# A graph kernel's opening: row statistics on ScalarE, row 0 placed ahead of the turnings of h0

## What is computed

```python
h = jnp.maximum(_layernorm(x, axis=-1), 0.0)
x = x + L0(h)       # three edge convolutions and a closing projection
h = jnp.maximum(_layernorm(x, axis=-1), 0.0)
x = x + L1(h)       # one weighted aggregation, normalised over the nodes

def _layernorm(x, axis=-1, eps=1e-05):
    m = jnp.mean(x, axis=axis, keepdims=True)
    v = jnp.var(x, axis=axis, keepdims=True)
    return (x - m) / jnp.sqrt(v + eps)

def _edge_conv(x, src, dst, W, b):
    xi = x[dst]
    xj = x[src]
    m = jnp.concatenate([xi, xj - xi], axis=-1) @ W + b
    s = jax.ops.segment_sum(m, dst, num_segments=N)
    cnt = jax.ops.segment_sum(jnp.ones((dst.shape[0],), m.dtype), dst, num_segments=N)
    return s / jnp.maximum(cnt, 1.0)[:, None]
```

## Time and profile before

| | us |
|---|---|
| median of 3 runs | 111.09 (110.65 to 111.28) |
| the profiled execution | 111.21 |
| its span | 109.4 |
| TensorE busy | 98.6 (90%) |
| its weight loads | 91.8 (84%) |
| VectorE busy | 87.9 (80%) |
| ScalarE busy | 63.8 (58%) |
| GpSimd busy | 20.8 (19%) |

### The profile page before, as it was taken

One profiled execution on the slowest core, in us unless ns is written; L12 is line 12 of the kernel. 1 busy time (PEld: TensorE's weight loads), 2 busy tenths in 40 slices (PEclk: granted clock), 3 DMA queues, 4 the chain that ended last, 5 costly groups with the idle time before them and its releaser, 6 DMA issues.

```text
span 109.4 us, 2712 instructions
## 1 busy us (share of the span) xinstructions
PE 98.6 (90%) x1050; PEld 91.8 (84%) x1050; DVE 87.9 (80%) x257; ACT 63.8 (58%) x154; POOL 20.8 (19%) x27
## 2 busy tenths in 40 slices
PE   0395999979999999999999999999999999999950
PEld 0333898867799989999999999999999999999840
DVE  2589999999999998999953599940999989808960
ACT  1595999998699989302858133557513153423540
POOL 7200000000000059100399920192000000000000
PEclk9999999999999999999999999999999999999999
DMA  1984930000030000000050200000000000000035
GB/s 28 260 186 93 328 115 0 0 6 3 3 99 0 6 0 9 6 0 3 0 192 13 88 0 0 6 0 0 0 6 0 0 0 0 0 0 6 0 76 158
DMA packets 7008, 4.63 MB, mean 42 GB/s; under 512 B 2175, under 2 KB 6994, under 8 KB 6994
## 3 DMA queue, kind: packets, MB, share of 16 engines
q1 hardware_dynamic: 6068, 3.68, 12.4%
q10 hardware_dynamic: 926, 0.75, 2.6%
HBM read 3.79 MB, written 0.64 MB: 40 GB/s over the span
## 4 chain that ended last, share of the span: by engine, by line
PE 72%; DVE 17%; DMA 5%; issue 1%; ACTq 1%; ACT 0%; DVEq 0%
PE bank L1385 14%; PE bank L1286 12%; PE bank L1142 12%; PE bank L1143 11%; PE bank L1144 11%; DVE src_hot L591 8%; DMA x_in<-in_x_dram 5%; PE bank L1216 4%; PE bank L1423 2%; PE bank L1363 2%; DVE stats L544 2%; DVE stats L864 1%; PE bank L1468 1%; DVE x_in L895 1%; DVE dst_hot L587 1%
## 5 line engine op out<-in xcount | busy, mean ns | idle before, releaser
L591 DVE TENSOR_SCALAR src_hot<-node_id,edge_cols 125x626 f16<-125x626 f16 x77 | 23.6, 379 | 0.0
L1286 PE MATMUL bank<-dst_hot,src_hot 125*128 125x84 f16 (+6 forms) x505 | 20.1, 195 | 1.3 <-DVE src_hot L591 1.1
L1286 PEld LDWEIGHTS bank<-dst_hot,src_hot 125*128 125x128 f16 x505 | 18.8, 98 | 2.8 <-DVE src_hot L591 1.8
L1385 PE MATMUL bank<-counts,u_lo 125*128 125x312 f32 (+3 forms) x60 | 16.7, 308 | 0.0
L1068 ACT ACTIVATE h_hi<-pre 128x312 fp32r<-128x312 f32 (+1 forms) x12 | 5.6, 466 | 16.4 <-DVE pre L757 16.4
L1385 PE MATMUL bank<-counts,u_hi 125*128 125x312 f32 (+3 forms) x48 | 14.0, 307 | 0.0
L1143 PE MATMUL bank<-wf_hi,h_lo 128*125 128x256 f32 x40 | 11.3, 281 | 0.0
L1142 PE MATMUL bank<-wf_hi,h_hi 128*125 128x256 f32 x40 | 11.3, 281 | 0.0
L1144 PE MATMUL bank<-wf_lo,h_hi 128*125 128x256 f32 x40 | 11.2, 281 | 0.0
L1385 PEld LDWEIGHTS bank<-counts,u_lo 125*128 125x128 f32 (+1 forms) x60 | 11.0, 189 | 0.0
L1003 ACT ACTIVATE parts<-bank 125x250 f32<-125x250 f32 x25 | 10.2, 411 | 0.0
(11 more groups left out here) (144 smaller groups left out, 250.0 us busy)
## 6 DMA issues: line engine op xcount, KB each, us to landing
raw<-in_L_gnn_W_dram SPq DMA_DIRECT2D x3, 512.0 KB, 6.6
x_in<-in_x_dram ACTq DMA_DIRECT2D x1, 560.0 KB
raw<-in_L_gnn_Wf_dram SPq DMA_DIRECT2D x1, 512.0 KB, 3.7
out_dram<-x_in SPq DMA_DIRECT2D x2, 168.0 KB
wf<-in_L_gnn_Wf_dram SPq DMA_DIRECT2D x1, 256.0 KB, 7.6
raw<-in_L_gnn_Wf_dram SPq DMA_DIRECT2D x1, 256.0 KB, 2.7
raw<-in_L_gnn_W_dram SPq DMA_DIRECT2D x1, 256.0 KB, 2.7
out_dram<-x_in SPq DMA_DIRECT2D x2, 112.0 KB
```

The lines of the kernel that those rows point to most:

```text
L591: dve.tensor_scalar(src_hot[:, t % RING, 0:IDS], node_id[:, 0:IDS], edge_cols[:, 0, t:t + 1], None, ALU.is_equal).then_inc(src_hot_vector, 1)
L1286: return pe.matmul(built[s][:, :, n0:n0 + n], src_hot[:, t % RING, BLK * s:BLK * s + P], dst_hot[:, c, :, j // 2, c0:c0 + n, j % 2], start ...
L1385: ins = pe.matmul(bank[KF * h + f][:, 0:e - a], u[0:n, k, P * f:P * (f + 1)], counts[0:n, k, a:e], start=False, stop=(k == NB - 1 and u is ...
```

## The change

- The statistics of x leave VectorE. ScalarE makes them with two activations a block that also write the sum of their output over the row: a copy scaled by 256^-1.5, whose sum is the mean over 16, and a square of (that mean minus x / 16), whose sum is the variance. They write their elements into `h0`, which is overwritten later. The shift is then made with -16 in place of -1.
- Source tiles 4, 22 and 27 are made by VectorE in place of ScalarE.
- On VectorE the reciprocal and the shift stand ahead of tile 15 (`NORM_AT`) in place of behind tile 1; the deviations come ahead of tile 9 in place of tile 5.
- TensorE places the whole of row 0 first. Behind it come the turnings 0, 1, 2, the products of blocks 0 and 1, the turnings 3 and 4, and the other products.
- Five warming products in place of ten.
- `centre` in the closing statistics waits for one count less, since the variances of x raise that semaphore no more.

```diff
@@ -62,9 +62,10 @@
 EPS = 1e-5
 
 FULL = 112
-SCALAR_EARLY, SCALAR_NEXT, SCALAR_LATER = (0, 4), (22, 27), {0: (34, 38), 1: (52,), 2: (71,)}
-SCALAR_TILES = SCALAR_EARLY + SCALAR_NEXT + sum(SCALAR_LATER.values(), ())
-DEV_AT, BAD_AT, VECS_AT, DIFF_AT = 5, 13, 26, 33
+SCALAR_EARLY, SCALAR_LATER = (0,), {0: (34, 38), 1: (52,), 2: (71,)}
+SCALAR_TILES = SCALAR_EARLY + sum(SCALAR_LATER.values(), ())
+DEV_AT, BAD_AT, VECS_AT, DIFF_AT = 9, 13, 26, 33
+NORM_AT = 15
 U_AT = (30, 38, 42)
 FLAG_AT = 62
 
@@ -324,6 +325,8 @@
         parts_copied = sem("parts_copied")
         weights_summed = sem("weights_summed")
         variance_ready = sem("variance_ready")
+        row_mean_ready = sem("row_mean_ready")
+        row_variance_ready = sem("row_variance_ready")
         std_ready = sem("std_ready")
         norm_ready = sem("norm_ready")
         h0_ready = sem("h0_ready")
@@ -550,14 +553,14 @@
                     last = dve.bn_aggr(moments[0:BLK, b, :], stats[0:BLK, b, :])
                 last.then_inc(variance_ready, 1)
 
-            def scale_shift(blocks, ready):
+            def scale_shift(blocks, ready, by=-1.0):
 
                 stds[0] += 1
                 dve.wait_ge(std_ready, stds[0])
                 lo, hi = blocks[0], blocks[-1] + 1
                 step.add(dve.reciprocal(rstd[0:BLK, lo:hi], rstd[0:BLK, lo:hi]))
                 step.wait()
-                dve.scalar_tensor_tensor(out=shift[0:BLK, lo:hi], in0=moments[0:BLK, lo:hi, 0], scalar=-1.0,
+                dve.scalar_tensor_tensor(out=shift[0:BLK, lo:hi], in0=moments[0:BLK, lo:hi, 0], scalar=by,
                                          in1=rstd[0:BLK, lo:hi], op0=ALU.mult, op1=ALU.mult).then_inc(ready, 1)
 
 
@@ -624,14 +627,10 @@
             dve.tensor_copy(weight_parts[:, :, :, 0:PER], p2).then_inc(weight_parts_ready, 1)
             dve.wait_ge(weight_parts_ready, 1)
             weighted_window(0)
-            dve.wait_ge(x_loaded, 32)
-            for b in range(NB):
-                moments_of(b)
-            variances(range(NB))
             dve.wait_ge(edge_cols_ready, 1)
-            source_tile(1)
-            scale_shift(range(NB), norm_ready)
-            for t in range(2, TILES):
+            for t in range(1, TILES):
+                if t == NORM_AT:
+                    scale_shift(range(NB), norm_ready, -math.sqrt(D))
                 if t == DEV_AT:
                     deviations()
                 if t == BAD_AT:
@@ -870,7 +869,7 @@
                             stats[:, 2 * f:2 * f + 2, :].rearrange("p a b -> p (a b)")).then_inc(variance_ready, 1)
 
             def centre(f):
-                dve.wait_ge(variance_ready, stds[0])
+                dve.wait_ge(variance_ready, stds[0] - 1)
                 step.add(dve.scalar_tensor_tensor(out=shift[:, f:f + 1], in0=moments[:, f, 0:1], scalar=vec(3, f),
                                                   in1=vec(3, f), op0=ALU.add, op1=ALU.subtract))
                 step.wait()
@@ -976,17 +975,25 @@
                 copy(h0_t[:, :, BLK * b:BLK * (b + 1)], t2).then_inc(h0_t_ready, 1)
 
 
-            root(rstd[0:BLK, 0:NB], moments[0:BLK, 0:NB, 1])
+            act.wait_ge(x_loaded, 32)
+            for b in range(NB):
+                nc.scalar.activation(h0[:, b, :], x_in[:, b, :], ACT.Copy, scale=D ** -1.5,
+                                     accum_out=moments[0:BLK, b, 0:1]).then_inc(row_mean_ready, 1)
+            for i, b in enumerate(range(NB)):
+                act.wait_ge(row_mean_ready, i + 1)
+                nc.scalar.activation(h0[:, b, :], x_in[:, b, :], ACT.Square, bias=moments[0:BLK, b, 0:1],
+                                     scale=-D ** -0.5, accum_out=moments[0:BLK, b, 1:2]).then_inc(row_variance_ready, 1)
+            act.wait_ge(row_variance_ready, NB)
+            nc.scalar.activation(rstd[0:BLK, 0:NB], moments[0:BLK, 0:NB, 1], ACT.Sqrt,
+                                 bias=eps[0:BLK, :]).then_inc(std_ready, 1)
             act.wait_ge(norm_ready, 1)
             for b in range(NB):
                 nc.scalar.activation(h0[:, b, :], x_in[:, b, :], ACT.Relu, bias=shift[0:BLK, b:b + 1],
                                      scale=rstd[0:BLK, b:b + 1]).then_inc(h0_ready, 1)
                 if 1 <= b < NB - 1:
                     h0_high(b - 1)
-            source_tile(SCALAR_NEXT[0])
             h0_high(NB - 2)
             h0_high(NB - 1)
-            source_tile(SCALAR_NEXT[1])
             high_rows(("u", 0, 0), 0, 2)
 
             def copy_block(r, s):
@@ -1170,7 +1177,7 @@
             ins.then_inc(filled, 1)
             pe.wait_ge(constants_ready, 3)
             pe.wait_ge(padding_ready, 1)
-            keep_warm(10)
+            keep_warm(5)
 
             def turn_dev():
                 pe.wait_ge(bad_ready, 1)
@@ -1261,8 +1268,6 @@
                 return pe.matmul(o[:, 0:e - a], degree_r[0:rows, :], part[0:rows, NB - 1, a:e], start=opens, stop=closes,
                                  skip_group_check=True)
 
-            jobs = {2: (0,), 4: (1,), 6: (2,), 9: (3, 4)}
-            assert max(jobs) < len(window_pieces(0))
             made = [0, 0]
 
             def wait_tile(t):
@@ -1290,10 +1295,6 @@
                 if r == 0:
 
                     for i in range(len(pieces)):
-                        if i == 8:
-                            neighbour_terms_0(U0_BLOCKS[:1])
-                        for b in jobs.get(i, ()):
-                            turn_h0(b)
                         wait_tile(seen)
                         seen += 1
                         for s in range(NB):
@@ -1322,6 +1323,11 @@
                             pe.wait_ge(flag_ready, 1)
                             general = pe.value_load(flag[0:1, 0:1], min_val=0, max_val=1)
                 if r == 0:
+                    for b in range(3):
+                        turn_h0(b)
+                    neighbour_terms_0(U0_BLOCKS[:1])
+                    turn_h0(3)
+                    turn_h0(4)
                     neighbour_terms_0(U0_BLOCKS[1:])
                 if r == 1:
                     own_terms_0()
```

## The result

The changed kernel takes **115.09 us** (median of 4, 114.95 to 115.14), the kernel before 110.89 in the same comparison: ratio 1.0367, 95% interval 1.0343 to 1.0391. It is slower, as forecast, but by 4.2 and not by 2.1, and lies 0.3 above the range. The profiled execution takes 115.14, its span is 113.0, 2.14 lie around it.

What follows compares the result with a forecast made beforehand. TensorE, busy for 90% of the span, was taken to bound the kernel; row 1 ending at 26.65 instead of 24.54 adds 2.1 to 111.21, giving 113.3, or 113.2 against the median 111.09; range 111.8 to 114.8 us.

Steps and rivals of the forecast that it cites:

- The direction and its mechanism: TensorE, opening: 5.63 of turnings and products left behind row 0, idle 0.87 and 0.37 for ScalarE's copies; 2.1 us slower.
- the first h0: ScalarE, after its statistics and the root: first h0 at 12.86 instead of 10.06.
- Writing the sum ... I take 0.15, ten times, 1.5: ScalarE's statistics: writing sums costs 0.15 each, 1.5 in all (0 to 3.0), on top of 3.35 for the activations.
- TensorE's clock: Rival, TensorE's opening: 1.2 GHz, hidden in row 0; 118.8 us if it lasts through turnings and products; chance 0.05.
- all 5.63 doubled: Clock rival's price: the turnings and products behind row 0, 5.63 of work, double at the low level, giving 118.8.
- Five end at 7.5. That is worth nothing in itself: TensorE's start: five warming products end at 7.5, no gain in itself, since row 0 goes at VectorE's pace.
- The chain after 24.54 shows no such room: After the own terms' old start: argument that nothing later can make up part of the 2.1 delay.
- the third rival: Something later, such as row 4, takes up at most 1.0: 112.2, or about 111.4 with cheap sums; chance 0.05.
- The time around the span: Outside the profiled span: 1.8 of the kernel before's 111.21; the forecast added only the 2.1 to that whole time.
- The stall at t = 15: VectorE at the normalisation: idle about 0.9, from 11.5 to 12.4, waiting for ScalarE's root.
- that for the high part of u: VectorE after its tiles at 18.3: idle about 1.9 until ScalarE has the high part of u of block 0.
- The wait for tile 34: TensorE in row 1: waits 0.35 for ScalarE's tile 34, ready at 24.75.

Runs made afterwards that it cites:

- the filled standstill: The changed kernel with seven unused products of 512 columns ahead of TensorE's wait for tile 15: 112.74 us, ratio 1.0152 to the kernel before.
- thicker placements: The changed kernel with one unused product of 256 columns ahead of each of tiles 2 to 14: 114.22 us, ratio 1.0297 to the kernel before.
- the order alone: The kernel before with row 0 placed ahead of the turnings and products, statistics, tiles and ten warming products as before: 116.89 us, ratio 1.0484.
- the same order: The changed kernel with turnings 0 and 1 ahead of tile 15 and turning 2 ahead of tile 17: 112.24 us, ratio 1.0117; 111.25 at clock 1.0.

## Why the prediction was wrong

- **The direction and its mechanism were right.** TensorE is behind with 5 turnings and 10 products when row 0 ends, and the copies in ScalarE's queue hold it up. At full clock (the filled standstill) the own terms start 1.6 later, where 2.1 was forecast; the 0.5 between them comes from the first h0, which is there 0.6 sooner than forecast.
- **"Writing the sum ... I take 0.15, ten times, 1.5"** was too dear: 0.09, so 0.9. With the last 0.1 and x landing 0.2 sooner, the first h0 came at 12.25, not 12.86, and row 0 ended at 14.65, not 15.2. Without the readings the activations are 0.31 and 0.40 apart; my 0.28 and 0.39 from the rows were a little low. The trace agrees with what I had estimated from the figures of the Trainium skill ("ScalarE: Activation LUTs", "What ACT_TABLE_LOAD costs"), 0.31 and 0.40.
- **The step that failed is "TensorE's clock", chance 0.05, "against it: the idle stretches before cost nothing".** What the runs show in its place is a fall to 1.2 GHz, from 14.0 to 20.8 in the profiled execution and with a mean clock of 0.97 in all four, worth 2.3 of the 4.2; the rival at 0.05 was the one that came. The idle stretches before did cost nothing, but there products of fp32 operands stood between them. The change takes out exactly these, and half of the warming products, and puts 4.5 of thin placements and a standstill of 1.67 in their place. The times that make the standstill stood in my working (VectorE at its wait until 12.4, then the windows), and I did not lay them beside the clock. The price was put at the extreme too, all 5.63 doubled; measured, the low level covered the turnings and the first products, 2.3. What exactly makes the clock fall stays open: filling the standstill holds it in every execution, ten warming products in three of four, thicker placements only delay the fall, and the order alone lets it fall in some executions and not in others. The high level went when work had been thin and had then stopped; in that direction the trace agrees with the rule of the Trainium skill ("TensorE: Matmul & The Clock Gate", "Part 1: The HAM clock gate") that the prediction names.
- **"Five end at 7.5. That is worth nothing in itself"** is wrong: in the kernel before five fewer warming products alone cost 1.3 in the median of ten executions (seven of them slower, three not), and with the change ten of them hold the clock in three executions of four.
- **"The chain after 24.54 shows no such room"** is wrong by 0.4: in the kernel before row 4 ended at VectorE's last tiles. This was the third rival, at a third of its price, and on top of the loss.
- **The time around the span was taken as constant;** it grew by 0.33. What in the statistics brings it is not known.
- The stall at t = 15 was 0.30 (forecast 0.9) and that for the high part of u 4.42 (1.9): the former by the cheap sums, the latter by the clock (with the standstill filled it is 2.12). The wait for tile 34 was 0.55 (0.35).

In sum, for the two profiled executions: 1.6 at full clock and 2.3 from the clock up to the own terms, less 0.39 in rows 2 to 4, plus 0.1 behind them, plus 0.33 around the span: 3.9. The medians are 4.2 apart, since the profiled execution of the kernel before was 0.3 above its median.

## What to carry to other kernels

Before moving work out of a waiting engine's gaps, list what the gaps then hold: on TensorE an emptied gap costs not only its own length but can cost the clock of what follows. A few unused products in the gap (four of 512 columns here) held the high level in all of twelve executions, and the time was that of the same order at full clock without them and with tile 34 on ScalarE (111.28 and 111.25). When the bound engine gains, read how far ahead the next one is at the places where they meet later: rows 2 to 4 took 15.9 where VectorE was ahead of TensorE and 16.3 where it was not, so 0.4 of a gain in row 1 can be lost there. And weigh the halves of a change with the clock held and as they run: the reordering on top of the statistics wins 0.5 with the clock held, by the estimate above, and loses 0.6 as run.

## What was unexpected of the hardware

- The clock fell to 0.50 behind a standstill of 1.67 that followed 4.5 of placements, and was there from 14.0 to 20.8, although TensorE had been busy again since 13.6; with thicker work before, it fell later and was back sooner, and with the order alone it fell behind a standstill of 0.97.
- The clock row does not show the low level before the first rise: fp32 passes took up to twice their time at a row of 9. The lengths of single placements show it, and that the rise came near 10.6 in one execution and near 9.6 in another with the same instructions so far.
- Reading a sum is an instruction of its own, 0.19 long, 0.09 in the queue.
- Versions with ScalarE's statistics spend 0.33 more outside the profiled span; neither the semaphores, the square, nor the sum readings alone do it.
